# Values at the end of the following step, scores and maxima ahead of them, and no full-array matmuls in the steps of two attentions

## What is computed

```python
# block 1 of 6: windowed attention, 8 images, 2 shifts x 2 strip directions, 8 heads of 8 channels
attn = softmax(einsum('whqc,whkc->whqk', qw, kw))        # 128 queries x 128 keys in a window
ow   = einsum('whqk,whkc->whqc', attn, vw) + lw
# block 3 of 6: attention over the 1024 tokens of an image, 16 heads of 8 channels, 8 images
attn = softmax(einsum('bhqd,bhkd->bhqk', q, k))
out  = einsum('bhqk,bhkd->bhqd', attn, v) @ w_proj + b_proj
```

## Time and profile before

| | us |
|---|---|
| median of 3 runs | 4560.41 |
| the profiled execution | 4556.71 |
| its span, first to last instruction | 4554.6 |
| window attention, steps | 335 to 925 |
| token attention, steps | 1272 to 3027 |

### The profile page before, as it was taken

One profiled execution on the slowest core, in us unless ns is written; L12 is line 12 of the kernel. 1 busy time (PEld: TensorE's weight loads), 2 busy tenths in 40 slices (PEclk: granted clock), 3 DMA queues, 4 the chain that ended last, 5 costly groups with the idle time before them and its releaser, 6 DMA issues. The chain is left out here.

```text
span 4554.6 us, 74651 instructions
## 1 busy us (share of the span) xinstructions
PE 3870.5 (85%) x25243; PEld 1648.1 (36%) x25243; DVE 2549.4 (56%) x4085; ACT 1923.6 (42%) x2321; POOL 840.2 (18%) x861
## 2 busy tenths in 40 slices
PE   7988888847698989898999999876997838999999
PEld 4655555524322212121222222224346723444444
DVE  3246555546577777777777777723447622333333
ACT  1215454511146565555555565643432312232332
POOL 0002222310000000000000000000430004555555
PEclk9989787978789999999999999987999859999999
DMA  4443343300400000000000000001430012322221
GB/s 142 133 109 88 91 88 85 80 16 2 165 9 14 18 14 18 13 18 14 18 14 20 12 23 18 4 8 56 151 102 1 0 72 80 94 83 76 97 81 48
DMA packets 137582, 247.79 MB, mean 54 GB/s; under 512 B 34808, under 2 KB 47264, under 8 KB 136800
## 3 DMA queue, kind: packets, MB, share of 16 engines
q1 hardware_dynamic: 137312, 243.98, 18.9%
HBM read 171.55 MB, written 56.62 MB: 50 GB/s over the span
## 5 line engine op out<-in xcount | busy, mean ns | idle before, releaser
L1071 DVE TENSOR_REDUCE mxv<-mx_ps 128x1 f32<-128x512 f32 x2048 | 1315.2, 685 | 413.8 <-PE mx_ps L931 413.5
L1046 ACT ACTIVATE PT<-st_ps 128x1024 f32<-128x1024 f32 x1024 | 1003.6, 1022 | 710.7 <-PE st_ps L943 710.5
L931 PE MATMUL mx_ps<-KS,QS 24*128 24x512 f16 x2048 | 731.7, 397 | 30.3 <-DMA QS<-qk 16.4
L957 PE MATMUL o_ps<-PT,VA 128*32 128x512 f32 x4096 | 559.6, 618 | 159.2 <-ACT PT L1046 107.9
L1914 DVE TENSOR_TENSOR u<-h_ps,s 128x512 f32<-128x512 f32 x352 | 243.3, 691 | 541.4 <-ACT s L1889 492.7
L1951 POOL TENSOR_TENSOR hg<-u,gb 128x512 f32<-128x512 f32 x352 | 451.5, 1284 | 378.7 <-DVE u L1914 300.9
L666 DVE TENSOR_REDUCE mxv<-mx_ps 128x4 f32<-128x512 f32 x512 | 332.9, 685 | 231.8 <-PE mx_ps L542 229.5
L1889 ACT ACTIVATE s<-h_ps 128x512 f32<-128x512 f32 x352 | 210.2, 597 | 595.4 <-PE h_ps L1863 595.4
L368 PE MATMUL st_ps<-KS,ident 128*128 128x512 f16 x1024 | 406.0, 396 | 6.8 <-ACT TX L1036 6.2
L1871 PE MATMUL y_ps<-hg,w 128*128 128x512 f32 x704 | 360.7, 596 | 56.3 <-POOL hg L1951 56.2
L943 PE MATMUL st_ps<-QS,KS 26*128 26x512 f16 x2048 | 404.4, 392 | 0.0
(11 more groups left out here) (231 smaller groups left out, 4399.0 us busy)
## 6 DMA issues: line engine op xcount, KB each, us to landing
gb<-g SPq DMA_DIRECT2D x64, 512.0 KB, 3.7
gb<-g SPq DMA_DIRECT2D x16, 2048.0 KB
QK<-qk SPq DMA_DIRECT2D x128, 192.0 KB
qk<-hl SPq DMA_DIRECT2D x80, 256.0 KB, 3.3
RB<-d SPq DMA_DIRECT2D x48, 256.0 KB, 3.5
qk<-hl SPq DMA_DIRECT2D x64, 128.0 KB, 3.3
v<-vs SPq DMA_DIRECT2D x32, 256.0 KB, 3.2
VS<-v SPq DMA_DIRECT2D x32, 256.0 KB, 3.1
```

What stands on the lines that cost most here:

```text
L931: nc.tensor.matmul(mx_ps[:, use % 3, :], rows(QS, g // 2, j, STACK)[:, t * C:(t + 1) * C], rows(KS, g // 2, j, STACK)[:, half * HALF:(half ...
L957: mm = nc.tensor.matmul(o_ps[32 * j:32 * j + 32, :], VA[:, g // 2 % 2, kt, j, :], PT[:, n % 2, j, :], start=(kt == 0), stop=(kt == KT - 1))
L1046: nc.scalar.activation(PT[:, n % 2, 2 * a:2 * a + 2], st_ps[:, a], ACT.Exp, scale=1.0 / SHIFT ** 2).then_inc(st_free[a], 1)
L1071: nc.vector.tensor_reduce(mxv[:, g % 2, j, t, half:half + 1], mx_ps[:, slot], AX.X, ALU.max).then_inc(mx_free, 1)
```

## The change

`fill_array` is gone and neither attention calls it. In both, the maxima of a pair of heads come behind the scores instead of around them, and `values(i, n - 1)` moves from the middle of step n to its end, behind the scores and maxima of both halves. The turn stays behind the maxima of the first half. Warm-up, waits, counts of slots and the other engines' streams are unchanged.

```diff
-def fill_array(nc, out, ident, rows):
-
-    nc.tensor.matmul(out, ident[:], rows, start=True, stop=True)
...
                 def scores(n, a):
                     u, s = n // 4, n // 2 % 2
-                    fill_array(nc, st_ps[:, a, 1], ident, KS[:, u, s, 0:HALF])
                     for w in range(4):
...
                         for a, pair in enumerate(PAIRS):
-                            ahead(pair[0])
                             pe.wait_ge(st_free[a], i * STEPS + (n + 1))
                             if n == WARM_AT and a == 0:
                                 warm_up(nc, st_ps[:, a, 0], identf, X)
                             scores(n, a)
-                            ahead(pair[1])
+                            for j in pair:
+                                ahead(j)
                             if a:
                                 continue
                             if n % 4 == TURN and (kind != "last" or u < 3):
...
-                            if n:
-                                values(i, n - 1)
-                            elif kind != "first":
-                                values(i - 1, STEPS - 1)
+                        if n:
+                            values(i, n - 1)
+                        elif kind != "first":
+                            values(i - 1, STEPS - 1)
```

More of the change, by code:

```diff
@@ L940, in scores @@
                     g, kt = n // KT, n % KT
-                    fill_array(nc, st_ps[:, a, 1], ident, KS[:, g // 2, 0:HALF])
                     for e in range(2):
@@ L1014, in image @@
                                 turn(use)
[L1015 to L1018, removed]
+                        if n:
+                            values(i, n - 1, kind)
+                        elif kind != "first":
+                            values(i - 1, STEPS - 1, "mid")
                 periods(pe, image)
```

## The result

| | before | after |
|---|---|---|
| median of the runs, us | 4556.75 (4 runs, 4534.22 to 4561.75) | 4789.14 (4 runs, 4785.15 to 4791.44) |
| span of the profiled execution, us | 4554.6 | 4789.6 |
| granted clock over the span | 0.918 | 0.712 |
| window attention, first values to last, us | 583 | 537 |
| token attention, first values to last, us | 1750 | 2018 |

The ratio is 1.0519 (95% interval 1.0482 to 1.0556). The forecast was 4750 us, inside the case "the clock falls and stays low"; the time is 39 us above it and inside that case's own range. For a few of the kernels further down the points at which the clock falls and rises differ from one execution to the next, so that their times spread by several per cent; their spread is given in place of an interval.

What follows compares the result with a forecast made beforehand. No engine is full; a loop over several engines sets the step (3.23 us token, 3.74 window). Token attention +236, window -35, less a few us for longer fast stretches: +193 on 4556.71, so 4750 us; range 4165 to 4830.

Steps and rivals of the forecast that it cites:

- the clock falls and stays low: Both attentions: 2.4 GHz for about 8 steps behind each warm-up, then 1.2; 4750 us, own range 4670 to 4830, chance 0.62.
- Part 1: Attention steps at 2.4 GHz in the new order: 2.58 us, with turns 2.66 (token) and 2.78 (window), against 3.23 and 3.74.
- Part 2: Fills of both attentions: each puts 0.32 us ahead of its scores at 2.4 GHz; removed, none is left in the step.
- Part 3: Attention steps at 1.2 GHz in the new order: 3.88 us, with turns 3.96 (token) and 4.08 (window).
- Which clock: Both attentions: without full-array fills and with 0.6 us idle per step, 2.4 GHz lasts about 8 steps behind each warm-up.
- Cannot win it back: Attention steps of before, once at 1.2 GHz, do not regain 2.4; each later fall lasts until the next image's warm-up.
- The sum: Token attention +236 us, window attention -35, less a few us for longer fast stretches: +193, giving 4750 us.
- SyncE's queue: Window attention, outside the sum: if the clock holds, TensorE's rows come up to 3 us late in some units.
- rival A: Both attentions: the clock holds at 2.4 GHz without fills; token -288 us, window -72, time 4197 us; chance 0.25.

Runs made afterwards that it cites:

- the fastest kernel: The changed kernel with one fill put back ahead of scores(n, 1) and the five f32 warm-up matmuls of each image removed; 4088.83 us, ratio 0.8985.

## Why the forecast was right, step by step

**Part 1, the fast step.** Right in size: 2.52 us against 2.58, with VectorE's slot in front of head 1, and the turn step 3.12 (1270.05 less the values at 1266.93), 0.60 more against 0.63. Its reading as a gain of the order was incomplete. Fast steps in all four cases: 3.23 before, 2.85 with the order alone, 2.54 with the fills' removal alone, 2.52 with both. The fills' removal alone brings the loop to VectorE's own 2.5, and the order then has 0.02 left to give. The order alone stops at 2.85, because one fill still lies in the loop; with that fill taken out and the other left it is 2.53.

**Part 2, the fills.** Right: one in the loop costs 0.33 us, against 0.32. What it did not ask is where the other stands. In the new order the fill ahead of scores(n, 1) is beside VectorE's reductions and costs nothing. So "none of that is left in the sum" was true, and only half of it was ever there to gain.

**Part 3, the slow step.** 3.83 us against 3.88; window steps 3.85 (values at 441.46 and 445.31) against 3.88.

**Which clock.** The side was right, and the reason that it rested on, full-array work, was borne out: 4158 us with a 128-row fill, about 4705 with a 24-row fill of the same columns, 4789 with none. The idle gap of 0.6 us in a step, which I counted beside it, is not enough for a fall: with one fill ahead of scores(n, 0) each step has it and the clock stays at 1.00 (4339 us). Without fills the fall came at or one step behind the gap of 1.02 us in seven of eight images; that gap was in no row that I had, and moving the reciprocal away from it was not tried. The number of fast steps was too high: eight forecast, and ten in the first image but two or three in the others (behind the warm-up at 1745.00 values at 1752.11, 1754.63 and 1757.83, then 1.94 us long). The Trainium skill, "TensorE: Matmul & The Clock Gate", section "HAM oscillation — how this bites in real kernels", names long idle gaps as what makes the clock fall. This trace again disagrees in part: the longest gap ahead of the fall at 1275 was 0.60 us.

"Cannot win it back" was wrong as a general statement, and it supported the forecast. The trace of before spoke against it already. Behind the stall at 525.47, with no warm-up near (the last one ahead is at 484.44), TensorE before the change:

```profile
530.94 1.93 PE L570 MATMUL o_ps<-PT,VA 128*32 128x128 f32 x32
...
534.65 0.39 PE L368 MATMUL st_ps<-QK,ident 128*128 128x512 f16 x1
...
536.17 1.08 PE L570 MATMUL o_ps<-PT,VA 128*32 128x128 f32 x32 [0.77 <-ACT OR L635]
```

So window steps of before won 2.4 GHz back some 7 us after its loss at 527.5 (here, too, a turn stood ahead of the rise, at 530.56), while the token steps without warm-ups mostly do so late (4606 to 4872 us). The new order with fills and without warm-ups takes 4 to 14 us. Of the changed kernel itself the statement was nearly right, and that its time came out near the forecast rests on this: between its warm-ups its token steps rose only behind the projection's full-array matmuls (at 1569.96, and lost at 1575.37 again, some 3 us after the rise), and once, about 3223.64, in the last steps, which have no maxima.

**The sum.** From one warm-up to the next an image takes 1745.00 - 1484.15 = 260.9 us (256 to 261 in the six images that can be measured so), forecast 252. Five slow steps more, 5 x 1.3 = 6.5, are most of that. The term that was mis-sized is thus the fast steps in the token attention: +236 forecast, +268 measured. The 8 us taken off for fast stretches longer than 8 steps went the wrong way. With the window attention at -46 for -35, and 13 us outside the two, that makes +235 for +193.

**SyncE's queue** was left out of the sum, with a price for the case in which the clock holds: rows late by up to 3 us in some window units. In the fastest kernel the window attention waits for them:

```profile
L558 PE MATMUL st_ps<-QK 26*128 26x128 f16 x2048 | 116.5, 239 | 81.6 <-DMA QK<-mT 60.2 <-issue 20.3 <-ACT PT L643 0.5
```

60.2 us of idle time end with the DMA of the rows QK<-mT, of a stage of 467 us; 6 us an image, 48 in all, was the price in rival A. This is now TensorE's largest single wait there.

## What to carry to other kernels

Before a matmul that nothing reads is taken out, ask two things of the timeline: does it lie in the loop or beside another engine's work, and what other matmuls use the whole array in that step. Move it under a wait before removing it; here that alone was the difference between 5% slower and 9% faster. Then measure whether the warm-up still earns its time, since a loop that keeps the array in use may bring the clock back by itself.

## What the runs showed that I had not expected

- Warm-up matmuls can cost more than they bring: 4158.31 us with, 4088.83 without, in the new order with one fill; the kernel before is the other way round, 4557 with and at best 4606 without.
- A step that differs in nothing but order recovers the clock within 14 us or, in four falls of five, not for 100 and more (new and old order, both with two fills, no warm-ups). Which feature of the order does it stays open; that five of the old order's six rises stand right behind a turn is the one lead in the traces.
- TensorE's busy share and its idle gaps do not tell whether the clock holds: 80% busy with gaps of 0.60 us held 2.4 GHz with a fill in each step, 86% over the span did not without.
- Taking one of two fills out of the old order cost 7.5%, more than taking out both (2.3%).
- A fill cut to 128 columns made the time vary by 8% between executions (4358 to 4728 us). A kernel whose steps only just keep the clock is not only slower but unsteady.
